# Windowed-attention layers of a three-phase tower: the two 42-column rests of the gated feed-forward computed as one tile

## The reference, cut to what matters

```
o = windowed attention of shift_token(x)            # q, k, v, 8 heads of 64, window 128
x = x + o @ wo
h = shift_token(x); h = normed(h) * lg + lb
h = h @ w1 + b1                                     # w1: 256 x 1364
a, g = jnp.split(h, 2, axis=-1)                     # 682 factors, 682 gates
h = a * jax.nn.gelu(g, approximate=False)
x = x + h @ w2 + b2                                 # w2: 682 x 256
```

## Time and profile before

| | before |
|---|---|
| median of 3 runs | 1368.27 us (1363.14 to 1372.32) |
| the profiled execution, its own time | 1366.47 us |
| its span, first to last instruction | 1364.7 us |
| PE matmul busy | 1241.3 us, 91% of the span |
| PE weight load busy | 1061.2 us, 78% |
| DVE busy | 970.3 us, 71% |
| ACT busy | 923.6 us, 68% |
| POOL busy | 634.0 us, 46% |
| mean granted clock of the PE | 0.968 of full speed |

### The profile page before, as it was taken

One profiled execution on the slowest core, in us unless ns is written; L12 is line 12 of the kernel. 1 busy time (PEld: TensorE's weight loads), 2 busy tenths in 40 slices (PEclk: granted clock), 3 DMA queues, 4 the chain that ended last, 5 costly groups with the idle time before them and its releaser, 6 DMA issues.

```text
span 1364.7 us, 26379 instructions
## 1 busy us (share of the span) xinstructions
PE 1241.3 (91%) x9057; PEld 1061.2 (78%) x9057; DVE 970.3 (71%) x2602; ACT 923.6 (68%) x2023; POOL 634.0 (46%) x697
## 2 busy tenths in 40 slices
PE   2799999999999993899966988999999999999986
PEld 2699889989988993677754657888888887888886
DVE  5767666666767646998776787678788778777532
ACT  2455765565576552888936769778778788888643
POOL 6523521452353214444333556556656657655433
PEclk9799999999999997999987999999999999999999
DMA  7300010010000004000010001100100000000010
GB/s 165 103 1 14 32 32 1 14 64 0 1 1 1 1 0 114 1 17 17 9 65 1 1 5 52 40 5 5 46 4 4 20 5 13 20 21 21 21 31 17
DMA packets 34881, 33.75 MB, mean 25 GB/s; under 512 B 11340, under 2 KB 31424, under 8 KB 34752
## 3 DMA queue, kind: packets, MB, share of 16 engines
q1 hardware_dynamic: 33856, 29.91, 7.1%
q0 software_dynamic: 768, 2.10, 0.9%
q10 hardware_dynamic: 128, 0.04, 0.0%
HBM read 25.75 MB, written 4.19 MB: 22 GB/s over the span
## 4 chain that ended last, share of the span: by engine, by line
PE 40%; ACT 8%; DVE 4%; issue 3%; POOL 3%; DMA 2%; SPq 1%; ACTq 0%; DVEq 0%; POOLq 0%
PE w_ring L1633 2%; PE w_ps_p L1663 2%; PE w_ring L1635 2%; PE w_ring L1634 2%; PE w_ring L1713 2%; PE a_ps L845 2%; PE w_ring L1714 2%; PE w_ring L1715 2%; PE w_ps_a L1681 2%; PE w_ring L1640 2%; DMA w_xs<-X 2%; PE w_ring L1725 2%; PE w_ps_d L1656 1%; PE w_ps_d L1653 1%; PE w_ring L1726 1%
## 5 line engine op out<-in xcount | busy, mean ns | idle before, releaser
L360 ACT ACTIVATE t_gf<-t_ps_f,t_fb_cur 128x512 f32<-128x512 f32 x128 | 87.9, 686 | 165.8 <-PE t_ps_f L280 164.2
L508 DVE TENSOR_TENSOR t_g_lo<-t_gf,t_g_hi 128x512 fp32r<-128x512 f32 x128 | 92.1, 721 | 81.5 <-ACT t_g_hi L362 80.5
L293 PE MATMUL t_ps_o<-t_w_hi,t_g_hi 128*128 128x256 f32 x512 | 145.8, 285 | 1.1 <-DVE t_g_lo L508 1.1
L295 PE MATMUL t_ps_o<-t_w_hi,t_g_lo 128*128 128x256 f32 x512 | 144.8, 283 | 0.0
L294 PE MATMUL t_ps_o<-t_w_lo,t_g_hi 128*128 128x256 f32 x512 | 144.8, 283 | 0.0
L1713 PE MATMUL w_ring<-w_nh,w_w_hi 128*128 128x256 f32 x384 | 113.3, 295 | 12.8 <-DVE w_gate L2241 6.2
L644 POOL TENSOR_TENSOR t_rs<-t_ve,t_neghalf 128x4 f32<-128x4 f32 x32 | 38.2, 1194 | 178.7 <-DVE t_ve L469 177.2
L2196 DVE COPY w_pt<-w_ps_p 128x384 f32<-128x384 f32 x128 | 70.5, 550 | 60.7 <-PE w_ps_p L1663 59.6
L278 PE MATMUL t_ps_f<-t_nh,t_w_hi 128*128 128x512 f32 x256 | 103.5, 404 | 6.9 <-DVE t_nl L607 3.6
L1714 PE MATMUL w_ring<-w_nh,w_w_lo 128*128 128x256 f32 x384 | 108.0, 281 | 0.0
L1715 PE MATMUL w_ring<-w_nl,w_w_hi 128*128 128x256 f32 x384 | 107.9, 281 | 0.0
(11 more groups left out here) (290 smaller groups left out, 4368.6 us busy)
## 6 DMA issues: line engine op xcount, KB each, us to landing
t_raw<-in_L_tok_w SPq DMA_DIRECT2D x8, 1024.0 KB
out<-X SPq DMA_DIRECT2D x14, 256.0 KB, 2.2
raw<-in_L_ffn_wqkv SPq DMA_DIRECT2D x2, 1536.0 KB, 6.8
raw<-in_L_ffn_w SPq DMA_DIRECT2D x4, 682.0 KB, 5.2
w_raw_o<-out SPq DMA_DIRECT2D x8, 256.0 KB, 3.0
w_xs<-X SPq DMA_DIRECT2D x16, 127.0 KB
w_raw<-in_L_ffn_w SPq DMA_DIRECT2D x2, 640.0 KB
t_raw_d<-in_L_tok_D SPq DMA_DIRECT2D x4, 256.0 KB
```

The costliest lines, as they stand in the source:

```text
L293: pe.matmul(out, g_hi[:, j % 4, tok], w2_hi[:, j, :], start=(j == 0 and t % 2 == 0), stop=False, skip_group_check=True)
L295: mm = pe.matmul(out, g_lo[:, j % 4, tok], w2_hi[:, j, :], start=False, stop=(j == FC - 1 and t % 2 == 1), skip_group_check=True)
L360: act.activation(gf[:, j % 2, :], ps_f[:, j % 2, :], ACT.Gelu, bias=fb_cur[:, j:j + 1]).then_inc(pf_free, 1)
L508: dve.tensor_tensor(g_lo[:, j % 4, :], gf[:, j % 2, :], g_hi[:, j % 4, :].bitcast(F32), ALU.subtract).then_inc(g_split, 1)
```

## The change

The rests of factors and gates are put side by side in the weight tile that held the gates' rest alone: the factors' 42 columns at columns 0 to 41 of tile j = 5 of u = 1, the gates' 42 at columns 64 to 105. One product then gives the factors' rest on PSUM partitions 0 to 41 and the gates' on 64 to 105, and the call of the factors with j = 4 makes one tile in place of two. ACT's sixth gelu call becomes two instructions: an Identity with bias that brings the factors' rest to a new SBUF tile `last_a`, then the Gelu, which reads partitions 64 to 105 and writes partitions 0 to 41. DVE's sixth `gated` multiplies two SBUF tiles. w1 is loaded with four DMAs per layer; the bias of the rest of the gates is loaded twice, at rows 0 and 64.

```
+    LAST, UP = HID - FULL, P // 2
-    NLOAD = 4 + 2 * (1 + 2 * L) + 4 * L
+    NLOAD = 4 + 2 * (1 + 2 * L) + 5 * L
...
                 for u in range(2):
-                    sp.dma_start(raw_1[:, :, u, 0:HID], w1[:, :, u, :]).then_inc(S["raw_1"], 16)
+                    sp.dma_start(raw_1[:, :, u, 0:FULL], w1[:, :, u, 0:FULL]).then_inc(S["raw_1"], 16)
+                for u in range(2):
+                    sp.dma_start(raw_1[:, :, 1, FULL + UP * u:FULL + UP * u + LAST], w1[:, :, u, FULL:HID]).then_inc(S["raw_1"], 16)
...
-                        sp.dma_start(b1_all[0:LAST, i, u, FC - 1:FC], b1[(FC - 1) * P:HID].rearrange("(p c) -> p c", c=1)).then_inc(S["vec"], 16)
+                        for row in range(0, UP * u + 1, UP):
+                            sp.dma_start(b1_all[row:row + LAST, i, u, FC - 1:FC], b1[FULL:HID].rearrange("(p c) -> p c", c=1)).then_inc(S["vec"], 16)
...
-                for j in (j, j + 1):
+                chunks = (j,) if u == 0 and j == FC - 2 else (j, j + 1)
+                for j in chunks:
...
-                act.wait_ge(S["raw_1"], 32 * l + 32)
+                act.wait_ge(S["raw_1"], 64 * l + 64)
-                act.activation(w1_hi[:, :, u, 0:HID], raw_1[:, :, u, 0:HID], ACT.Copy).then_inc(S["hi_1"], 1)
+                cols = slice(0, FULL + (UP + LAST) * u)
+                act.activation(w1_hi[:, :, u, cols], raw_1[:, :, u, cols], ACT.Copy).then_inc(S["hi_1"], 1)
...
+                if j == FC - 1:
+                    l = f // NSQ
+                    act.activation(last_a[0:LAST, :], ring[0:LAST, RB[b], STOK:2 * STOK], ACT.Identity, bias=b1_all[0:LAST, l, 0, j:j + 1])
+                    act.activation(gate[0:LAST, j, :], ring[UP:UP + LAST, RB[b], STOK:2 * STOK], ACT.Gelu,
+                                   bias=b1_all[UP:UP + LAST, l, 1, j:j + 1]).then_inc(S["gelu_done"], 1)
+                    return
...
+                if j == FC - 1:
+                    dve.tensor_tensor(gate[0:LAST, j, :], last_a[0:LAST, :], gate[0:LAST, j, :], ALU.mult).then_inc(S["gated"], 1)
+                    return
...
                 for w in (w1_hi, w1_lo):
-                    dve.memset(w[:, :, :, HID:HIDP].bitcast(F32), 0.0)
+                    dve.memset(w[:, :, 1, FULL + UP + LAST:HIDP].bitcast(F32), 0.0)
+                dve.memset(gate[:, FC - 1, :], 0.0)
...
+                cols = slice(0, FULL + (UP + LAST) * u)
-                pool.tensor_tensor(w1_lo[:, :, u, 0:HID], raw_1[:, :, u, 0:HID], w1_hi[:, :, u, 0:HID].bitcast(F32), ALU.subtract).then_inc(S["split_1"], 1)
+                pool.tensor_tensor(w1_lo[:, :, u, cols], raw_1[:, :, u, cols], w1_hi[:, :, u, cols].bitcast(F32), ALU.subtract).then_inc(S["split_1"], 1)
```

More of the change, by code:

```diff
@@ L1397, in window_phase @@
     HIDP = FC * P
-    LAST = HID - (FC - 1) * P
+    FULL = (FC - 1) * P
+    LAST, UP = HID - FULL, P // 2
     IC = INNER // P
@@ L1454, in window_phase @@
         gate = sb("gate", [P, FC, STOK])
+        last_a = sb("last_a", [P, STOK])
         nf = gate[:, 0:DC, :]
@@ L1714, in hidden_in @@
                         pe.matmul(dst, w1_lo[:, c, u, cols], nh[:, c, :], start=False, stop=False, skip_group_check=True)
-                        mm = pe.matmul(dst, w1_hi[:, c, u, cols], nl[:, c, :], start=False, stop=(j % 2 == 1 and c == DC - 1), skip_group_check=True)
+                        mm = pe.matmul(dst, w1_hi[:, c, u, cols], nl[:, c, :], start=False, stop=(j == chunks[-1] and c == DC - 1), skip_group_check=True)
                 mm.then_inc(S[full], 1)
@@ L2238, in gated @@
             def gated(f, j, b):
+                dve.wait_ge(S["gelu_done"], FC * f + j + 1)
+                if j == FC - 1:
+                    dve.tensor_tensor(gate[0:LAST, j, :], last_a[0:LAST, :], gate[0:LAST, j, :], ALU.mult).then_inc(S["gated"], 1)
+                    return
                 dve.wait_ge(S["a_full"], FC // 2 * f + j // 2 + 1)
-                dve.wait_ge(S["gelu_done"], FC * f + j + 1)
                 dve.scalar_tensor_tensor(gate[:, j, :], ring[:, RB[b], j % 2 * STOK:(j % 2 + 1) * STOK], b1_all[:, f // NSQ, 0, j:j + 1], gate[:, j, :],
```

## The result

| | before | after |
|---|---|---|
| median, first comparison (20 runs of each) | 1368.10 us | 1360.55 us |
| ratio, 95% interval | | 0.9953 (0.9937 to 0.9970) |
| median, second comparison (24 and 12 runs) | 1366.96 us | 1362.10 us |
| ratio, 95% interval | | 0.9965 (0.9948 to 0.9982) |
| profiled execution: own time, span | 1366.47, 1364.7 | 1357.90, 1356.2 |

The changed kernel is 0.4% faster, 5.6 us by the mean of the two ratios (1 - 0.9959, times 1367 us). The forecast was 1360.3 us and -8.0 us. One of the twenty runs before took 6594 us; it is a slow one, and the ratios leave it out.

The account below looks back on a forecast made before the run. PE was taken as the bound in phase three's ordinary halves. Terms -8.5 - 1.8 - 0.2 - 0.2 + 1.65 + 1.1 gave -8.0 us, 1360.3 us on the median, with 8 in 10 between 1354 and 1367.

Parts of the forecast that it names:

- Matmuls removed, -8.5 and -1.8: Six matmuls fewer per step on PE: 0.71 us in each of twelve ordinary halves, 1.8 us in the last four.
- The Identity, +1.65: Extra ACT instruction, 0.38 us at each of four late places, plus 0.13 for a wider split of w1's gates.
- The cover: In an ordinary half, 0.68 us between the end of ACT's `keep_values` and PE's start, hiding the Identity's 0.38, even 0.57.
- The rival of the broken cover: ACT's added time per step exceeds the cover, through table loads or slow cross-partition reads: slower, 1397 us with loads; chance 0.04.
- places of rows 5: Four PE waits, at 853.85, 967.28, 1108.35 and 1261.03 us, that go back to ACT's run; each 0.4 us longer.
- DVE's 3.44 us: A tiny DVE tensor_scalar beside a long POOL instruction; its wait might fall away, with up to 1.8 us of PE's wait.
- the rival of the charges: ACT's 1.65 and the bias's 1.1 hidden, or DVE's long wait gone: 1355.8 to 1357.6 us; chance 0.14.
- The sixth multiply, 0: DVE's sixth `gated` on two SBUF tiles: taken as nothing, with 1.6 us kept in the range for waits beside POOL.
- The bias's DMAs, +1.1: Two more bias DMAs on SP's queue delay DVE in phase two, at 534.99 us, by 2 x 0.54 us.
- the smaller zeros: Memsets of fewer columns, on the chain: -0.2 us.
- Another engine closes the half: The loop through ACT, DVE and POOL is as long as PE's, so 8.5 us falls away: 1368.8 us; chance 0.11.
- it doesn't do what it says: The matmuls would still be there, or a one-tile call's start costs what it saves: 1370 us; chance 0.03, with all else.

Follow-up runs that it names:

- matmuls_only: The kernel before, with the factors' call with j = 4 leaving out its second tile, six matmuls; 1356.79 us, ratio 0.9930 to the kernel before.
- no_identity: The changed kernel without the Identity on ACT, last_a set to zero once; 1357.87 us, ratio 0.9931 to the kernel before.
- identity_x2: The changed kernel with one more Identity, on 32 partitions, on ACT in each step; 1369.06 us, ratio 1.0016 to the kernel before.
- matmuls_back: The changed kernel with the factors' j = 4 call again issuing twelve matmuls, six of them never read; 1370.46 us, ratio 1.0036 to the kernel before.
- bias_two_late: The changed kernel with the two added bias DMAs moved behind SP's wait for the table; 1361.65 us, ratio 0.9951 to the kernel before.

## Why the prediction was right, point by point

**Matmuls removed, -8.5 and -1.8.** Right. 0.71 us per ordinary half by the distance of starts, where the duration of 0.28 would have given 6 x 0.28 = 1.7; the body of matmuls_only has 8.2 of 8.5. The whole, 10.3, was measured as 10.5 and 9.6. The tail's 1.8 alone was seen in one profile (92.1 to 90.3), not in the other (93.7), and not in matmuls_only (92.6); it isn't shown by itself.

**The Identity, +1.65.** The four places were right; the sum was too small. The Identity itself takes 1.4 us, 1.2 at the four places and 0.2 at a fifth. What else is new in ACT's run, which no_identity keeps, was forecast at 0.13 and is 0.3 before the wait of the first half, 0.5 at 1104.65 (0.84 less 0.31) and 0.3 at 1254.91. Against matmuls_only the changed kernel is behind by 0.58 us up to the end of POOL's wait in the first half and by 1.85 in the eleven others: 2.4 us in the body, where 1.65 - 0.2 = 1.45 was forecast. The mis-sized step is "the Identity on 42 partitions has the same 256 columns, so I take 0.38": the spacing of like instructions was taken for one whose neighbour starts at other rows. The run grew by 0.45 in an ordinary half, within the bounds of 0 and 0.57, and by 0.70 where the split of w1 stands behind the gelus.

**The cover.** "0.68 us of cover, which hides 0.38 and even 0.57" held by a hair: 0.08 us remain, and identity_x2 shows that 0.65 more is paid in every half. "Even 0.57" is wrong: 0.15 of the cover went elsewhere, which the forecast did not have, and with 0.57 the rest would have been overdrawn. The rival of the broken cover, at 0.04, had its price right (0.68 us and then everything) and stood nearer than the forecast's 0.3 made it look.

**Waits at the places of rows 5, "0.4 longer".** Mostly wrong as a sign to look for. 853.85 and 967.28 kept their lengths (2.62, and 1.81 against 1.88). At the first an earlier wait, at 845.16, took the growth (0.22 us before at 844.00, now 0.83). At the second the 0.4 is there against matmuls_only (1.81 against 1.42), and the new wait for DVE in front hides it. 1261.03 grew by 0.17 and 1108.35 by 0.84. A loss moves to the wait that comes first on the same chain.

**DVE's 3.44 us, in the rival of the charges.** At its old place it fell away, as that rival had it possible: the same instruction takes 0.42 now. But the wait moved on, to two later instructions of DVE. They take 1.03 and 1.89 us, where they took 0.17 each before, and each ends 0.03 us behind an instruction of POOL.

```profile
1137.37 0.42 DVE L2239 TENSOR_SCALAR w_ve<-w_mv 128x2 f32<-128x2 f32 x1
...
1140.34 1.03 DVE L2180 TENSOR_TENSOR w_ya<-w_y 128x16 f32<-128x16 f32 x1 [1.77 <-ACT w_y L1956]
1141.41 1.89 DVE L2182 SCALAR_TENSOR_TENSOR w_yb<-w_ya,w_sc 128x16 f32<-128x16 f32 x1
```

PE no longer waits for DVE there, but of its 1.8 us 1.33 remained, now for ACT's `keep_values` in the same half. The half gave 0.90 where matmuls_only, with the wait for DVE intact, gave 0.73: of 1.8 us that the rival had counted, 0.2 came.

**The sixth multiply, 0, and a wait beside POOL.** Right for the changed kernel: its sixteen take 0.40 us each, the longest 0.41, in place of 0.48. But it was a matter of 0.3 us. In the half of 932 us the multiply starts at 931.91 us and POOL's split of the q, k and v weights at 932.25. In `matmuls_back` the order is the other way round, and the multiply, one of sixteen, takes 2.55 us. DVE and POOL there:

```profile
932.53 2.55 DVE L2260 TENSOR_TENSOR w_gate<-w_last_a,w_gate 42x256 f32<-42x256 f32 x1
```

```profile
932.42 2.38 POOL L2414 TENSOR_TENSOR qkv_lo<-raw,qkv_hi 128x1024 fp32r<-128x1024 f32 x1 [0.77 <-ACT qkv_hi L1934]
```

PE lost 0.2 us in that half. The Trainium skill's rule (SBUF — State Buffer, Who interferes with whom) that DVE with two SBUF inputs contends with a GpSimd instruction that reads SBUF speaks of this form, and this trace agrees. The forecast had followed a half in which POOL was idle when tile 5 comes; in a half with a weight split it isn't. The 3.44 us are another case: a tensor_scalar has a single SBUF input, and by the forecast's words it would have been free. The same section of the Trainium skill frees an instruction with one SBUF input only outside the 2-port modes, and names tensor_scalar among those that can enter them; which mode it ran in no trace here shows.

**The bias's DMAs, +1.1.** The place was right, the term too small there: 1.9 us at DVE. How much of it reaches the end isn't settled.

**The sum.** With the charges as the traces have them, 2.4 in the body, 0.5 to 1.9 in phase two and 0.3 saved by the smaller zeros (from the first memset to that of `mx` it is 0.92 us, where it was 1.21), it is between -10.3 + 2.4 + 0.5 - 0.3 = -7.7 and -6.3 us; 5.6 was measured, and the two intervals together reach from 2.5 to 8.6. The stretches of clock, 1.5 us in the changed kernel's favour at 856 and 1.2 to 1.4 against it at 700 (most of it won back by 810), are not in that sum. The forecast of -8.0 has its charges too low, by 0.3 to 1.7 us by the traces and by 1.6 to 2.5 by the times above. That its 1360.3 fits 1360.55 so closely, and 1362.10 nearly, is in part luck of where those medians fell.

**Closing rivals.** "Another engine closes the half" is refuted by both matmul kernels; "it doesn't do what it says" by the 352 matmuls. Fourteen gelu loads, all of 1283 ns as in the earlier trace rows, stand in the changed trace too, so Identity needed none.

## What to carry to other kernels

Price a removed instruction by the distance of starts where its engine is the bound, and then ask at which engine the half would close next and how far off that is: here 0.71 us were taken from the PE, and 0.60 of the 0.68 us that ACT had were spent, so a further instruction on ACT has 0.08 us left per half. Whether ACT would hold back a further saving on the PE wasn't tried. An ACT instruction on 42 or 32 partitions was no shorter than one on 128, and it cost its neighbours their overlap. An instruction of DVE that has to wait out one of POOL may be free in one version and cost 2 us of DVE's time in the next, by which of them comes first. Small loads that are needed late should not stand before a wait that is needed early: moving ten of them brought 3.6 us, at the edge of the noise, beside the 5.6 of the whole change.

## What the hardware did that I had not expected

In the kernels read here ACT overlaps neighbours in PSUM-to-SBUF instructions of 256 columns (0.36 us apart for 0.47 of duration) only where their first rows agree, and all that agreed were at row 0; else they stand 0.48 to 0.49 apart, and the split behind them starts later too. 42 or 32 partitions take 0.46 to 0.47 us, as 128 do.

The granted clock of the PE differs between executions of one kernel, behind its waits, and each such stretch moves what follows by 1 us and more. The tail of the changed kernel and of its second profile, from 1320 to 1340 us:

```profile
1320.00:1340.00 20.00, 13.71 (x100) 13.28 (x100) 5.22 (x14) 8.06 (x20) 7.46 (x9) 0.91 0.05 17
```

```profile
1320.00:1340.00 20.00, 13.97 (x88) 13.39 (x88) 5.23 (x14) 7.90 (x19) 7.50 (x9) 0.81 0.06 18
```

That is 100 against 88 matmuls in the same 20 us. The one execution with a granted clock of 0.973 in the mean took 1352.81 us, another of the same kernel (bias_two_late) 1365.91. A profile of one execution is exact for positions between two waits, and no measure of a whole time to better than some 5 us.
